# A gated delta-rule layer and a mixture of experts: the causal convolutions of Q, K and V moved from VectorE into TensorE matmuls

## The reference, cut to what matters

```python
def _causal_dwconv(x, w, b):          # x: tokens x 1024 channels, w: 1024 x 4 taps
    y[t, c] = sum_j w[c, j] * x[t - 3 + j, c] + b[c]      # written here as a sum
    return silu(y)
q = _causal_dwconv(x @ Wq, qcw, qcb)  # 16 heads of 64 channels
k = _causal_dwconv(x @ Wk, kcw, kcb)
v = _causal_dwconv(x @ Wv, vcw, vcb)
q, k = rope(q), rope(k)               # then both are normalised per head
o = delta_rule(q, k, v, alpha, beta)  # a recurrence over the tokens, per head
x = x + (g * silu(norm(o))) @ Wo      # g = x @ Wg
x = x + second_block(layernorm(x))    # softmax attention, then 2 of 8 experts
```

## Time and profile before

| | us |
|---|---|
| median of three runs (7070.91 to 7072.53) | 7071.67 |
| time of the profiled execution | 7069.69 |
| its span, first to last instruction | 7067.6 |
| a turn with all streams (start to start) | 215.0 |
| PE busy / DVE busy / ACT busy / POOL busy | 5137.7 / 4870.4 / 3485.1 / 2615.7 |
| mean granted TensorE clock, as a share of 2.4 GHz | 0.776 |

### The profile page before, as it was taken

How to read it: one execution, slowest core, us unless ns; L and a number is a source line. 1 busy time by engine, 2 the same in 40 slices (tenths; PEclk the granted TensorE clock), 3 DMA queues, 4 the chain that set the end, 5 groups by cost and what they waited for, 6 DMA issues and landing times.

```text
span 7067.6 us, 126933 instructions
## 1 busy us (share of the span) xinstructions
PE 5137.7 (73%) x40448; PEld 3663.3 (52%) x40448; DVE 4870.4 (69%) x11585; ACT 3485.1 (49%) x5995; POOL 2615.7 (37%) x2957
## 2 busy tenths in 40 slices
PE   3677777777767777777777677777777777777776
PEld 2455555555545555555555455555455454555555
DVE  5667777667776677776677776677766777767752
ACT  2345554545554545545555545455444555455533
POOL 3444333344333444333443334343333433334420
PEclk6677877777877878777778778777777787777777
DMA  1000010000010100110000101000100001000001
GB/s 47 8 20 25 24 34 30 28 26 27 27 34 27 31 22 24 34 34 24 28 25 27 34 27 31 25 28 26 34 27 28 25 24 34 30 28 28 25 25 44
DMA packets 214675, 199.48 MB, mean 28 GB/s; under 512 B 13848, under 2 KB 176416, under 8 KB 209696
## 3 DMA queue, kind: packets, MB, share of 16 engines
q1 hardware_dynamic: 213920, 190.01, 8.9%
HBM read 148.02 MB, written 4.19 MB: 22 GB/s over the span
## 4 chain that ended last, share of the span: by engine, by line
PE 41%; issue 23%; DVE 19%; ACT 10%; POOL 6%; DVEq 1%; ACTq 0%; DMA 0%; SPq 0%; POOLq 0%
PE bank L1039 38%; DVE acc L1433 3%; PE bank L1043 3%; DVE NP L1575 3%; DVE tmpb L1602 2%; DVE mx L1684 2%; DVE Gam L1566 2%; ACT acc L854 2%; POOL fo L716 1%; ACT h L1026 1%; ACT L883 1%; POOL QK L816 1%; POOL nrm L728 1%; DVE Gam L1605 1%; ACT acc L877 1%
## 5 line engine op out<-in xcount | busy, mean ns | idle before, releaser
L1039 PE MATMUL bank<-QK 64*128 64x256 f32 (+1 forms) x4096 | 858.2, 427 | 628.9 <-DVE NP L1575 298.3
L1433 DVE SCALAR_TENSOR_TENSOR acc<-bank,conv_w,acc 128x255 f32<-128x255 f32 (+2 forms) x2304 | 931.8, 473 | 379.7 <-ACT acc L854 197.5
L1039 PEld LDWEIGHTS bank<-QK 64*128 64x128 f32 (+1 forms) x4096 | 358.1, 173 | 1059.4 <-issue 378.1
L1026 ACT ACTIVATE h<-bank,b 128x256 f32<-128x256 f32 x1024 | 415.8, 473 | 611.2 <-PE bank L1039 607.5
L854 ACT ACTIVATE acc<-bank,conv_b,conv_w 128x256 f32<-128x256 f32 x512 | 260.8, 559 | 868.6 <-PE bank L1039 716.3
L1039 PE MATMUL bank<-mT,W 128*128 128x256 f32 x2048 | 665.5, 483 | 24.4 <-DMA W<-in_W 22.6
L789 POOL TENSOR_TENSOR frstd<-fmv,neg_half 128x2 f32<-128x2 f32 x96 | 66.8, 696 | 1350.7 <-DVE fmv L1416 1350.7
L1039 PEld LDWEIGHTS bank<-mT,W 128*128 128x128 f32 x2048 | 502.2, 255 | 121.1 <-DMA W<-in_W 24.1
L1039 PE MATMUL bank<-W,h 128*128 128x128 f32 x4096 | 515.7, 280 | 55.4 <-DVE QK L1701 51.4
L810 POOL TENSOR_TENSOR sq<-acc 128x256 f32<-128x256 f32 x256 | 186.4, 728 | 973.7 <-ACT acc L860 973.7
L1039 PEld LDWEIGHTS bank<-W,h 128*128 128x128 f32 x4096 | 490.9, 194 | 105.6 <-DVE QK L1701 63.0
(11 more groups left out here) (227 smaller groups left out, 11769.9 us busy)
## 6 DMA issues: line engine op xcount, KB each, us to landing
W<-in_W SPq DMA_DIRECT2D x512, 256.0 KB, 2.9
QK<-QK SPq DMA_DIRECT2D x32, 1024.0 KB, 5.4
xin<-in_x SPq DMA_DIRECT2D x32, 128.0 KB, 2.2
x<-in_x SPq DMA_DIRECT2D x32, 128.0 KB, 2.2
xnG<-xnT SPq DMA_DIRECT2D x32, 128.0 KB, 2.0
out<-moe SPq DMA_DIRECT2D x32, 128.0 KB, 2.0
NP<-in_c_alpha_sel SPq DMA_DIRECT2D x1, 1024.0 KB, 5.0
Wqkv<-in_Wq SPq DMA_DIRECT2D x1, 512.0 KB, 6.1
```

The costliest lines, as they stand in the source:

```text
L1026: ins = s.activation(h1[:, n % 2, f, :], ps[:, q, :], ACT.Gelu_apprx_tanh, bias=b1[:, n, f:f + 1])
L1039: return mm(out_, lhsT, rhs, start=first, stop=last)
L1433: v.scalar_tensor_tensor(acc[:, n % 2, m, j:T], ps[:, m, 0:T - j], conv_w[:, kind, c, PAD - j:KT - j], acc[:, n % 2, m, j:T], ALU.mult, AL ...
```

## The change

1. **Weights.** On the chip, before the first turn, each of the 24 half weights (3 kinds x 4 taps x 2 halves, 128x512) is multiplied by its tap of each channel: POOL or DVE writes diagonals (`diagonal`), PE spreads them over all partitions (a product with `ones`), DVE multiplies (`scaled`), and SP stores them in a DRAM tensor `taps`. From there SP loads, each turn, four pieces of 512 KB for V (`V_piece`) and eight of 512 KB for Q and K (`QK_piece`) into two buffers each, every piece after the products two steps before it.
2. **Convolutions.** `("qk", n)` is 2 kinds x 4 taps = 8 products of 128x256 accumulated in the bank, from `xnT` shifted (it now has three zero columns ahead). `("v", m)` is, for each of two token blocks, 4 products with the tokens as weights and `V_taps` streaming, and one more that adds the bias: 10 products of 128x256, already with tokens on the partitions.
3. **After them.** ACT applies silu with the bias straight from the bank (`silu`, `values`). `first_tap`, `taps`, silu in place, the turned step and the copy of V go.
4. **Placement.** `SIDE` is a new table: among others Q and K come at blocks 16 to 27 instead of block 15 to the join stage, and the softmax attention (`max`, `att`, `pv`) later, half of it in the join stage. V's four steps move from head 10, block 0 and block 2 to head 7, head 11, block 1 and block 10. `xln` moves from head 2 to head 11.
5. **SP's order** now follows the side table. `alpha_sel` is a column that is broadcast; some tiles share memory (`sumsT` lies in `rot`, `ctxn` in `hn`).

The diff's core (line numbers are not kept):

```diff
-            return [(("qk", n), "v_conv", 6 * (n + 1), CONV_BANK)]
+            return [(("qk", n), "a_silu", n + 1, CONV_BANK)]
@@ placement, some lines of the table
-    (("head", 2), steps("attn", ("silu", 0), ("silu", 1)) + steps("front", ("xln", 0))),
+    (("head", 11), steps("attn", ("fqk", 0)) + steps("experts", ("down", 1)) + steps("front", ("xln", 0))
+      + steps("V", ("v", 1))),
+    (("block", 17), steps("front", ("silu", 0)) + steps("experts", ("up", 6)) + steps("front", ("qk", 1))),
@@ weights, once
+            for n in range(NTAPS):
+                pe.wait_ge(diag_v if n % 3 == 2 else diag_p, ...)
+                product(banks[n % 4][:], ones, spread[:, 512 * (n % 3):512 * (n % 3) + 512]).then_inc(spread_t, 1)
+                v.tensor_tensor(scaled(n), raw[:, kind, 512 * half:512 * half + 512], banks[n % 4][:], ALU.mult)
@@ SP
+            def QK_piece(c):
+                sp.dma_start(QK_taps[:, c % 2].rearrange("p a j n -> p (a j n)"), taps[4 + c])\
+                    .then_inc(QK_in[c % 2].sem, 16)
+                elif step == "qk" and not (n >= NC - 2 and ends(k)):
+                    hold(*full_at(k, ("qk", n)))
+                    QK_piece((n + 2) % NC)
@@ PE
-                    for q in range(2):
-                        c = 2 * m + q
-                        ins = product(ps[:, q, :], Wqkv[:, 2, c * P:(c + 1) * P], xnG[:])
+                    for t in range(NT):
+                        for j in range(KT):
+                            product(ps[:, t, :], xnG[:, j + t * P:j + (t + 1) * P], V_taps[:, m % 2, j, :], j == 0, False)
+                        ins = product(ps[:, t, :], ident[0:NC // 2, m:m + 1].to_broadcast([NC // 2, P]), V_bias[:], False, True)
+                    pe.wait_ge(QK_in[n % 2].sem, QK_in[n % 2].at(k, 16 * (n // 2 + 1)))
                     for kind in range(2):
-                        ins = product(ps[:, kind, :], Wqkv[:, kind, n * P:(n + 1) * P], xnT[:])
+                        for j in range(KT):
+                            ins = product(ps[:, kind, :], QK_taps[:, n % 2, kind, j, :], xnT[:, j:j + T], j == 0, j == PAD)
@@ ACT
-                    ins = s.activation(acc[:, n % 2, kind, :], ps[:, kind, :], ACT.Identity,
-                                       bias=conv_b[:, kind, n:n + 1], scale=conv_w[:, kind, n, PAD:KT])
-                s.activation(acc[:, n % 2], acc[:, n % 2], ACT.Silu).then_inc(a_silu.sem, 1)
+                    ins = s.activation(acc[:, n % 2, kind, :], ps[:, kind, :], ACT.Silu, bias=conv_b[:, kind, n:n + 1])
@@ DVE
-            def taps(i, use, n, which, began, taken):
-                for j in range(1, KT):
-                    for m, (kind, c) in enumerate(which):
-                        v.scalar_tensor_tensor(acc[:, n % 2, m, j:T], ps[:, m, 0:T - j], ...
```

More of the change, by code:

```diff
@@ L167 @@
[L167 to L182, removed]
@@ L205 @@
-    (("o", 0), steps("attn", ("fWo", 0))),
-    (("cross", 1), steps("front", ("silu", 7))),
-    (("o", 1), steps("front", ("rope", 6))),
-    ("end", steps("attn", ("mT", 0)) + steps("front", ("rope", 7)) + steps("attn", ("router", 0), ("wT", 0),
-      ("b2", 0)) + steps("front", ("sums", 0))),
+    (("head", 1), steps("attn", ("norm", 0), ("silu", 0))),
+    (("head", 2), steps("front", ("stat", 0)) + steps("attn", ("silu", 1)) + steps("experts", ("up", 0))),
+    (("head", 3), steps("attn", ("yT", 0))),
@@ new lines @@
+    (("block", 27), steps("attn", ("mrow", 0), ("mrow", 1)) + steps("front", ("qk", 7)) + steps("attn", ("mrow", 2),
+      ("mrow", 3)) + steps("front", ("rope", 5), ("silu", 7), ("rope", 6)) + steps("attn", ("att", 0), ("att", 1))
+      + steps("experts", ("down", 7)) + steps("attn", ("att", 2))),
+    (("block", 30), steps("attn", ("att", 3), ("att", 4)) + steps("front", ("rope", 7)) + steps("attn", ("pv", 0),
+      ("att", 5), ("att", 6), ("att", 7))),
+    ("join", steps("attn", ("att", 8), ("pv", 1))),
@@ new lines @@
+    (("top", 0), steps("attn", ("att", 9))),
+    (("low", 0), steps("attn", ("att", 10), ("att", 11))),
+    ("S", steps("attn", ("context", 0))),
+    (("o", 0), steps("attn", ("att", 12), ("pv", 2))),
+    (("top", 1), steps("attn", ("att", 13))),
+    (("cross", 1), steps("attn", ("att", 14), ("att", 15))),
+    (("low", 1), steps("attn", ("pv", 3), ("context", 1))),
+    (("o", 1), steps("attn", ("ctx", 0), ("ctx", 1), ("ctxT", 0), ("fWo", 0)) + steps("front", ("sums", 0))),
+    ("end", steps("attn", ("mT", 0), ("router", 0), ("wT", 0), ("b2", 0))),
@@ new lines, in row, with ends, back @@
+            def row(index, ahead):
+                return index + ahead if isinstance(index, int) else index[0] - index[1] + ahead
+            def ends(index):
+                return isinstance(index, int) and index == B - 1
+            for n in range(2):
+                QK_piece(n)
+            for n in range(2):
+                V_piece(n)
+            for n in range(2):
+                expert(n)
+            def back(k, meanwhile):
+                hold(xnT_ready.sem, xnT_ready.at(k, 1))
+                if begun(k, 0):
+                    hold(*full_at(turn(now[0])["attn"], ("g", 1, 1)))
+                sp.dma_start(xnG[:], xnT[:]).then_inc(xnG_in.sem, 16)
+                hold(v_QK.sem, v_QK.at(k, NC))
+                if begun(k, 0):
+                    hold(*full_at(turn(now[0])["attn"], ("QS", 1)))
+                sp.dma_start(QK1[:], QK[:, 1]).then_inc(QK1_in.sem, 16)
@@ new lines, in attn, with experts @@
+            def attn(j, step, n):
+                if step == "b2" and not ends(j):
+                    hold(v_moe.sem, v_moe.at(j, 1))
+                    sp.dma_start(x1[:], x_rows(row(j, 1))).then_inc(x1_in.sem, 16)
+            def experts(m, step, e):
+                if step == "down":
+                    if not (e >= NE - 2 and ends(m)):
+                        hold(*full_at(m, ("h1", e, 1)))
+                        hold(*full_at(m, ("y", e)))
+                        expert((e + 2) % NE)
+                    if e == NE - 1:
+                        hold(v_moe.sem, v_moe.at(m, v_moe.per))
+                        sp.dma_start(out_rows(row(m, 0)), moe[:]).then_inc(out_stored.sem, 16)
```

305 lines of the change are left out of this document (145 added, 160 removed).

## The result

| | before | after |
|---|---|---|
| median | 7072.1 us (7070.91 to 7074.39) | 7176.62 us (7149.73 to 7240.85) |
| ratio, with its 95% interval | | 1.0163 (1.013 to 1.0195) |
| span of the profiled execution | 7067.6 us | 7239.1 us |
| its first step of `back` in the first and the last turn | 88.6, 6695.4 us | 107.8, 6863.7 us |
| 31 turns / what follows | 6606.8 / 372.2 us | 6755.9 / 375.4 us |

The change made the kernel 1.6% slower; I had forecast 6930 us, 2% faster. Its times are also further apart: 7240.85, 7185.51, 7167.74 and 7149.73 us went with mean granted clocks of 0.814, 0.823, 0.824 and 0.827. Of the 171.5 us in the two profiled executions, 19.2 are ahead of the first turn, 149.1 in the 31 turns and 3.2 behind them.

The account below looks back on a forecast made before the run. No engine bounded the whole: DVE paced the block stage, DVE and PE alternated in the head, PE's chain led the join; the change moves the limit to PE. 7067.6 + 40 - 170 - 8 - 4 = 6926, forecast 6930 us, range 6760 to 7210.

Parts of the forecast that it names:

- The join stage: Last stage of a turn: Q and K chunks and sums go, half the softmax attention comes; -1.7 us, between +2 and -5.
- The head stage: First stage of a turn: more exposed PE work +6.7, against xn -3.7, gate log series -3.6, tap step -1.0; sum -1.6 us.
- The block stage: Middle stage of a turn: limit moves from DVE (58 us) to PE (72 us); 78.5 us against 80.7, -2.2.
- The V steps: V products at heads 7 and 11: 20 instructions each, 4.3 us at the upper clock, exposed in the head stage.
- V at the lower clock: Rival, head stage: V's products run at 1.2 GHz, 4.3 us more each, all exposed; 7197 us, chance 0.20.
- Late pieces: Rival: 512 KB weight loads land late, six of eight chunks wait 1.7 us, +10 per turn; 7240 us, chance 0.08.
- Once: Ahead of the turns: making the tap weights 31 us, plus uncovered stores and loads 9; +40 us (25 to 60).
- The turns that fill and empty the pipe: Two filling turns have little other PE work, -8 us; the last turns have no Q and K, -4.
- Better: Rival: busier PE keeps its clock up for old head and join work, 6 us more per turn; 6740 us, chance 0.12.

Follow-up runs that it names:

- the one-tap run: Kernel after plus four dense products before the first top product, each Q and K chunk making only the last tap's product: 6693.35 us in one run.

## Why the prediction was wrong, by its own steps

- **The join stage** is the step that failed: "I take -1.7, between +2 and -5". It took +10.5 (67.8 to 78.3, means of 24 turns). I counted the chunks and sums that leave as a gain of 5.6 us and held the clock of the rest as it was, 0.80; it was 0.59 on average. With four dense products at the stage's start, or with one chunk moved back, the time comes back (58.7 and 67.7 us), so the clock is the loss; which of the moves gave it up, chunks, `sums` or attention, is open. At a clock of 0.88 the same stage is 58.7 us, 9.1 less than before, more than my -5. A part of that is the clock, higher than the 0.80 of before; a part may be that DVE (38.6 to 18.7 us busy), ACT and POOL lost more than I had counted; the runs don't split it. `hn`, to which I gave nothing back, takes 0.60 us instead of 4.41, as it no longer runs beside POOL's two normalising steps.
- **The head stage**: forecast -1.6, measured -2.0. `xn` at 0.59 us is right; its move is worth 2.6 of the 3.7 us.
- **The block stage**: forecast 78.5, measured 77.6, by the wrong engine. PE did what I said: busy 70.65 us (72 forecast), a chunk in 3.7 us (3.5 forecast), clock 0.99. DVE was not 58 but 67.3 us, and set the pace. Of the 9 us, 6.5 are the solver (29.0 against 22.5 us). Two errors met at one number, which is luck; the one-tap run alone tells them apart.
- **The V steps**: 5.1 us each (20 instructions), forecast 4.3 to 4.4. The clock was up for them, so "V at the lower clock", whose 7197 us lies near the result, is wrong all the same: its mechanism, a clock that doesn't rise, struck in the stage where I had put no rival. The row to ask was in the earlier trace rows: the join stage's mean clock was 0.80 with the dense work in it, and I gave no price to its falling.
- **Late pieces** didn't occur: no chunk and no V step waits for its weights, which land in 3.2 us. What PE waits for a DMA, 29.9 us in all, is for expert weights.
- **Once**: making the weights took 24.0 us on PE (31 forecast), and the first transposes of `xn` come 25 us later (40 forecast). The eight first chunks then run every 4.7 us instead of every 5.5, and from those transposes to the first step of `back` it is 52.8 us instead of 58.6, which gives 6 back: +19. The turns that fill and empty the pipe gave nothing (-12 forecast): the first two took 391.9 us instead of 380.7, and what follows the start of the last took 3 more.
- **Better** was right in its kind: with the clock kept up, the span is 6664 us, 31 turns of 200.0 us. It doesn't come from the change alone.
- **The range** begins at 6760 us and is said to go from the better case, which the rival itself puts at 6740. The result lies inside the range near its other end, 7210, by luck: V at the lower clock had set that end.

## What to carry to other kernels

Don't carry a stage's clock over to other work: when dense products are moved out of a stretch of small ones, price the rest at 1.2 GHz too, as a rival, and read the mean clock of that stretch, not the page's. If the clock falls, a few idle dense products where PE waits anyway can win more than they cost (here four won 7.2%, two at the same place 2.8%, four some 8 us later 5.5%). They are no gift everywhere: at the start of a turn and in the kernel before they won nothing. And when work moves on POOL, look at which DVE operations now run beside it.

## What the runs showed of the hardware that I had not expected

- PE busy for 38.2 of 39.5 us with fp32 products of 64 to 128 columns (128x64, 64x64, some 128x128), and some of 256 over 32 columns of the array, stayed at a granted clock of 0.50. Sixty 64x64 products, 13.1 us, did not raise it, four products of 128x256 did. The Trainium skill ("TensorE: Matmul & The Clock Gate", "What's actually happening") says that the clock is set by how busy PE has been; busy time as the profile counts it doesn't decide here.
- With the same instructions, the stretch at the lower level came in a few lengths (24 or 31, 51 and 72 us, with join stages of 64 to 67, 76 and 83 us, once 80). The kernel's times spread over 91 us (before: 3.5), the longer the lower their mean clock. With four dense products between `join1` and `join2` they spread over 8.
- The bias product of V has only 4 rows, but costs more than a full one, 0.31 us per instruction against 0.23:

```profile
3149.42 1.89 PE L1084 MATMUL bank<-V_taps,xnG 128*128 128x256 f32 x8
3151.24 0.69 PE L1084 MATMUL bank<-V_bias,ident 4*128 4x256 f32 x2
3151.87 1.99 PE L1084 MATMUL bank<-V_taps,xnG 128*128 128x256 f32 x8
```

Its weights are one column, broadcast; whether that is the reason wasn't tried.
